# A PSUM copy moved within the evicting engine's round: graph transformer on one Trainium2 core

## The reference

```python
k = typed_linear(x, ntype, Wk).reshape(n, H, HS)      # q and v likewise; H = 8, HS = 16
kT = jnp.einsum('nhd,htdo->nhto', k, Watt)            # 32 edge types per node and head
vT = jnp.einsum('nhd,htdo->nhto', v, Wmsg)
kw = kT[src, :, etype]
m = vT[src, :, etype]
a = jnp.einsum('ehd,ehd->eh', kw, q[dst]) * pri[:, etype].T / SQRT_D
att = edge_softmax(a, dst, n)
hag = segment_sum(m * att, dst)                       # shapes left out
h = jax.nn.silu(typed_linear(hag, ntype, Wa))
h = h * alpha + x * (1.0 - alpha)                     # then a layer norm with g and b
```

## Time and profile before

| | |
|---|---|
| runs, median (lowest to highest) | 3823.72 us (3821.57 to 3826.46) |
| profiled execution, its own time | 3831.7 us |
| its span | 3829.7 us |
| busy: TensorE matmul, VectorE, GpSimd, ScalarE | 67%, 71%, 67%, 45% |
| joined stage, layer 0: first store of the table to last landing | 107.7 to 652.5 us |
| joined stage, layer 1: the same | 1873.4 to 2431.6 us |

### The profile page before, as it was taken

One profiled execution on the slowest core, in us unless ns is written; L12 is line 12 of the kernel. 1 busy time (PEld: TensorE's weight loads), 2 busy tenths in 40 slices (PEclk: granted clock), 3 DMA queues, 4 the chain that ended last, 5 costly groups with the idle time before them and its releaser, 6 DMA issues.

```text
span 3829.7 us, 61710 instructions
## 1 busy us (share of the span) xinstructions
PE 2556.1 (67%) x14673; PEld 1803.2 (47%) x14674; DVE 2719.9 (71%) x6690; ACT 1723.3 (45%) x3944; POOL 2562.5 (67%) x2612
## 2 busy tenths in 40 slices
PE   2777777366666666665577777556766676666587
PEld 1333333255555555554333333245555555555465
DVE  5666666577777777777577777667777777777654
ACT  1666666333333333333467666623343343343332
POOL 3666655677777777772666665577777777776266
PEclk8889888577777767767788889766776766677555
DMA  7999997545545444444799999655554444444222
GB/s 143 360 379 392 409 406 319 155 134 135 136 133 137 135 133 138 135 132 114 223 403 362 386 415 407 215 142 136 139 134 134 134 134 134 139 135 123 74 73 52
DMA packets 302264, 777.66 MB, mean 203 GB/s; under 512 B 69179, under 2 KB 229979, under 8 KB 289423
## 3 DMA queue, kind: packets, MB, share of 16 engines
q0 software_dynamic: 111152, 651.90, 48.6%
q1 hardware_dynamic: 182067, 121.18, 12.4%
q10 hardware_dynamic: 8704, 0.54, 0.2%
HBM read 335.05 MB, written 568.60 MB: 236 GB/s over the span
## 4 chain that ended last, share of the span: by engine, by line
POOL 42%; PE 20%; issue 17%; DMA 9%; ACT 6%; DVE 4%; SPq 1%; DVEq 0%; POOLq 0%; ACTq 0%
POOL region L759 40%; PE bank L1052 10%; DMA relation_table<-region,scatter_node 7%; ACT region L833 4%; PE bank L1073 2%; PE bank L1082 2%; ACT arena L851 1%; PE bank L1170 1%; PE bank L1169 1%; DMA region<-relation_table,key_of 1%; DVE sums L1673 1%; PE bank L1214 1%; PE bank L1168 1%; PE bank L1151 1%; DVE region L1474 1%
## 5 line engine op out<-in xcount | busy, mean ns | idle before, releaser
L759 POOL DMA_INDIRECT region<-relation_table,key_of x1664 | 1638.5, 985 | 519.2 <-issue 502.7
L1214 PE MATMUL bank<-region,arena 128*128 128x136 f32 x3328 | 736.5, 387 | 422.4 <-DVE region L1658 337.7
L1214 PEld LDWEIGHTS bank<-region,arena 128*128 128x128 f32 x3328 | 626.8, 273 | 515.4 <-DVE sums L1673 281.8
L1052 PE MATMUL bank<-sums,arena 128*128 128x512 bf16 x2048 | 666.4, 433 | 289.7 <-ACT region L833 258.9
L1474 DVE COPY region<-bank 128x512 f32<-128x512 f32 x896 | 589.4, 687 | 307.2 <-PE bank L1052 224.5
L950 ACT ACTIVATE arena<-iota_free,minus_dst 128x128 f32<-128x128 f32 x1664 | 528.5, 388 | 544.5 <-PE bank L1214 539.1
L833 ACT COPY region<-bank 128x512 f32<-128x512 f32 x1152 | 618.0, 609 | 136.8 <-PE bank L1052 106.9
L1200 PE MATMUL bank<-region_q,arena 128*128 x4992 | 579.6, 277 | 85.3 <-DVE arena L1644 79.2
L1636 DVE TENSOR_TENSOR region<-bank,region 128x512 f32<-128x512 f32 x416 | 287.3, 691 | 470.5 <-DMA region<-relation_table,key_of 451.0
L1200 PEld LDWEIGHTS bank<-region_q,arena 128*128 128x128 bf16 x4992 | 500.1, 126 | 157.9 <-issue 99.7
L1673 DVE TENSOR_TENSOR sums<-sums,bank 128x136 f32 x1664 | 475.4, 286 | 76.0 <-DVE sums L1673 46.1
(11 more groups left out here) (238 smaller groups left out, 2876.4 us busy)
## 6 DMA issues: line engine op xcount, KB each, us to landing
arena<-edge_places SPq DMA_DIRECT2D x416, 128.0 KB, 3.3
region<-relation_table,key_of POOLq DMA_INDIRECT x1664, 3.2
arena<-segment_flags SPq DMA_DIRECT2D x104, 128.0 KB
sums<-q_rows SPq DMA_DIRECT2D x6, 768.0 KB, 7.3
aggregated_rows<-sums SPq DMA_DIRECT2D x6, 768.0 KB, 5.2
sums<-relation_weight_parts SPq DMA_DIRECT2D x32, 128.0 KB, 8.6
x_sorted<-arena SPq DMA_DIRECT2D x16, 256.0 KB, 12.1
region_q<-x_sorted SPq DMA_DIRECT2D x16, 256.0 KB, 10.1
```

The source lines that it names most:

```text
L759: pool.indirect_dma_start(out=rows[:, block_.r, q * QUAD + s], out_offset=None, in_=table, in_offset=bass.IndirectOffsetOnAxis(ap=key_of[: ...
L1052: nc.tensor.matmul(bank[TABLE_BANK + k % TABLE_BANKS][:, :], x_spreadT[:, k, :], w_rel[:, k, :], start=True, stop=True).then_inc(table_psu ...
L1214: ins = nc.tensor.matmul(bank[SUM_BANK[q % 2][pair]][:, s * SUMC:(s + 1) * SUMC], onehots[:, at, 2 * pair + s], rows[:, block_.r, slot, RH ...
```

## The change

On ScalarE, `keep_qkv` of tile n+3 stood behind the sixth eviction of round n. Now `keep_qkv` of tile n+2 stands behind the fourth. Each tile's copy is made once, as before, in the round after the one that it was made in; `keep_qkv` itself and all other engines' streams are unchanged.

```diff
                     if tile.real:
                         evict(tile, ACT_HEADS[2:4])
+                    if tile.shift(2).real:
+                        keep_qkv(tile.shift(2))
                     if l and tile.j in (1, 2) and coming.real:
                         scale_res(0, g_res, coming.g, coming.gpar, coming.g // 2, (2 * tile.j - 2, 2 * tile.j - 1))
                     if tile.real:
                         evict(tile, ACT_HEADS[4:6])
-                    if tile.shift(3).real:
-                        keep_qkv(tile.shift(3))
                     if l == 0 and tile.n in REL_CAST:
                         cast_of(1, REL_CAST.index(tile.n))
                     if tile.real:
                         evict(tile, ACT_HEADS[6:])
```

## The result

The changed kernel takes 3791.55 us (median of 4 runs, 3789.1 to 3794.25) against 3825.09 us beside it: a ratio of 0.9914, 95% interval 0.9896 to 0.9931, or 33.5 us less, where 36 were forecast. A second measurement on another occasion gave 3793.6 against 3827.02 us, 0.9917 (0.9900 to 0.9934).

What follows compares the result with a forecast made beforehand. The joined stages were taken as within 3 to 4% of what the DMA engines carry. Stages 30, heads 2 and tails 4 us made 36 us less: 3823.7 to 3788 us, 0.9% less, range 3768 to 3818.

Steps and rivals of the forecast that it cites:

- forecast stage gains: Joined stages of both layers: fuller DMA share wins 15 of 16 us in layer 0, 15 of 22 in layer 1.
- rounds with a gate: Layer 1 rounds with a gate between heads 2 and 4: store misses by 1 to 2 us, 7 us lost over seven.
- Tails: From each layer's last landing to the end: 3.5 us saved in layer 0, 0.8 in layer 1, taken as 4.
- Heads: Start of each joined stage: first table store 1.2 us earlier, less 0.4 us in layer 1, taken as 2.
- (c): Rival: all the DMA room is won, and the tails, 38 + 7, up to 52 us: 3772 to 3779; chance 0.15.
- The store hence gains nothing in its own round: GpSimd's table store goes 9.2 us after its round's start, against 8.92 and 10.50 us in two rounds before.
- what improves is the pitch: Time per round: GpSimd needs 6.6 us for one round of all its steps, against 8.0 and more before.
- The 9.2 us: Predicted time from a round's start to the issue of its table store on GpSimd, 3.6 + 5.6 us.
- rival (b): Slower: table store stands behind the copy; at 12 us, 1 us more at 11 tiles per layer, 3840; chance 0.08.
- It waits a few tenths at most: TensorE's q, k, v matmul between heads 11 and 12, awaiting the copy that ends 3.3 us into the round.
- The rule of the Trainium skill: HBM share of about 358 GB/s binds between HBM and SBUF; would leave heads and tails alone, 6 us.
- The ceiling of 435: Fabric ceiling of the DMA transfers; would put layer 0's floor at an estimated 497 us, not 528.

Runs made afterwards that it cites:

- experiments 2: Changed kernel with the copy for the tile two ahead behind the second eviction instead of the fourth; 3793.17 us, 0.9913 to the kernel before.
- experiment 3: Changed kernel with the copy for the tile two ahead placed ahead of the first eviction; 3797.9 us, 0.9918 to the kernel before.
- experiment 9: Kernel before with the copy for the tile two ahead behind the sixth eviction and TensorE's q, k, v matmul behind heads 12 to 15; ratio 0.9990.
- 12: As experiment 9, with GpSimd's q store of a tile moved behind the next table store; 0.9936 to the kernel before.
- 1: Kernel before with the copy made for the tile two ahead but kept behind the sixth eviction; 3822.62 us, 0.9984 to the kernel before.
- experiments 1 to 8: Follow-up runs on copy place, gather order, half table bytes, a later table store and the changed kernel again; kernel before beside them, 3824 to 3829 us.
- experiment 11: Kernel before with x_sorted and h_sorted laid out so each partition's four rows are one 2 KB piece; 0.9995 beside 4386.36 us.
- experiment 6: Changed kernel with half the bytes of each table store; 3552.57 us, 0.9281 to the full kernel before.

## Why the prediction was right, and where it was not

**Right, with its mechanism.** The transfers bind the changed kernel: shares of 0.98 and 0.99, 439 us of waits for landings in both engines instead of 94, and 240 us for the same edit once half of their bytes are gone. What the engines gain is 1.83 us a round, what the kernel gains is the room the transfers had. The forecast stage gains were 15 and 15 us; from first store to last landing it was 11.0 and 17.7, the sum 28.7 for 30. That the sum is so close is partly luck: layer 0 fell 4 us short and layer 1 gave 3 us more. In layer 0 the share came to 0.98, not 0.99 and more. In layer 1 I had set aside 7 us for rounds with a gate, and experiments 2 and 3, which move such stores earlier and gain nothing, show no such loss. Tails: 3.6 us for 4. Heads: the first store of layer 0 is 1.4 us earlier, for a forecast of 1.2, but that is luck too: its round starts 1.2 us earlier, ahead of anything the change does, and the store comes only 0.2 us sooner after it (12.96 to 12.76). In layer 1 it comes 1.9 us sooner after its round's first eviction (13.62 to 11.68), for 0.8. The low end of the range, 3768, is called the far end of (c), whose own sum gives 3772; nothing hangs on it.

**The step that was mis-read.** "The store hence gains nothing in its own round", and "what improves is the pitch". The 9.2 us were right, 9.21 and 9.28 on the mean. But the mean of before is 9.80 and 10.25, so the stores do gain 0.6 and 1.0 us, and that counts beside the pitch: experiment 9 has the short engine round and stores at 10.9 us, and gains nothing; moved to 9.6 us (12) they give 24 us. How much belongs to which can only be estimated. On straight lines between the stretches of 12 and 9, short rounds at the old latenesses would give about 542 and 556 us: of the 14.5 us that the stretch of layer 0 lost some 11 are the pitch's and 4 the lateness's, of the 20.4 of layer 1 some 9 and 12. No run has the one without the other at these values. I had compared one round of 8.92 with one of 10.50 and taken the first. Had the copy's place cost 1.7 us more of lateness, the engines would have had their short round and the time would not have moved. The text did hold the number that decides: rival (b) put the point at which a store costs what it costs now at about 11 us behind the round's start, and 10.9 us is where experiment 9 came out even. What rival (b) missed is that the old place (1) lies on it already.

**"It waits a few tenths at most"** for TensorE's q, k, v matmul is right in the new place: the waits view gives it 34.2 us in 70 times for L851, 0.5 us each and 0.3 us a round. It hangs on the place, between heads 6 and 8: one pair of evictions later it is 1.76 us. So the tile two ahead needs the place as well. The place alone cannot be had, by the code and not by a run: a copy for the tile three ahead between heads 6 and 8 would wait for transposes that stand behind heads 12 to 15, and those wait for evictions behind the copy.

**The rule of the Trainium skill.** By the Trainium skill, "DMA: Bandwidth & Descriptors", section "Specifications", the HBM share of about 358 GB/s would have left only heads and tails. The trace disagrees: the changed kernel moves 405 and 404 GB/s over its two stages. The ceiling of 435 is not met over any longer stretch either: 422 in a window of 38 us is the most that was read, though single slices of 13 us show up to 443.

**What stays open.** Why the share stops at 0.98 to 0.99. A part can be placed in layer 0 of the changed kernel. The deepest dip, a share of 0.58 from 402.5 to 407.0 us, lies around the store of tile 34 (405.06 us), and the tile before it holds one node (its type has 385, by the reference's inputs); a smaller one, 0.89 from 272.5 to 274.5 us, lies at the store of tile 19 (272.54 us), behind a tile of four nodes. From 407 to 605 us the share is 1.00, at 414 GB/s. So nearly empty tiles, which the prediction reckoned with, seem to make part of the loss, but experiment 3 keeps it with its earlier stores, and no run shows the reason. Open too is why layer 1 began 3 us early beyond the 15.0 us that layer 0 gave, with an edge stage between that no edit touches.

## What to carry to other kernels

When an engine's wait is removed in front of a queue that is nearly full, two numbers decide and both must be read: the room of the queue (the share that is missing times its stretch), and the time from the landing that frees a buffer to the issue of the next transfer, on whichever engine issues it. A copy that moves by one place moves everything that is queued behind it on the consumer's engine too; here GpSimd's split, q store and gather carry the copy's time straight to the table store. To learn whether a stage is held by its transfers, halve the bytes; to learn whether the issue is late, move the issue alone.

## What the runs showed of the hardware that was not expected

The same kernel before takes 3824 to 3829 us in the measurements of the result and of experiments 1 to 8, and 4386 and 4363 us on two other chips, and the joined stages are not the reason: in experiment 11 their stretches are 548.7 and 562.1 us. Windows from the end of layer 0's joined stage to the start of layer 1's, of the kernel before, and of experiment 11 on the chip with 4386 us:

```profile
673.40:1859.80 1186.40, 739.09 (x4691) 609.98 (x4692) 860.64 (x2347) 427.89 (x1126) 843.01 (x855) 0.71 0.50 135
```

```profile
669.60:2126.50 1456.90, 734.17 (x4688) 599.65 (x4690) 853.95 (x2348) 429.43 (x1126) 837.45 (x856) 0.69 0.41 110
```

The busy times agree within 2%, the stretch is 270 us longer, and in it all engines idle more. VectorE's first use of the gathered table rows (L1636) waits 228.3 us there in the kernel before, for the gathers, and 411.1 us on the slower chip, for a releaser that this trace does not name. Whether the gathers land later is not recorded, and the cause is open. Ratios were taken on one chip each.

The granted clock was 1.00 in both stages of experiment 6, where TensorE is busy 354 of 400 and 358 of 420 us, and 0.88 and 0.87 before, where it is busy 401 of 545 and 429 of 558. Its two levels are 2.4 and 1.2 GHz. In the kernel before it falls again and again: TensorE idles 1.93 us up to 333.32 us, and from 335.2 to 338.6 us the granted clock is 0.50, the lower level. Four matmuls of heads there, and the next four, at the upper level again:

```profile
336.87 1.87 PE L1052 MATMUL bank<-sums,arena 128*128 128x512 bf16 x4
...
339.22 1.03 PE L1052 MATMUL bank<-sums,arena 128*128 128x512 bf16 x4
```
